# Recurrent attention: one fp32 exponential on ScalarE, and both fp16 terms of it made on VectorE

## The chip, the cores and the metric

The kernel runs on one core of a Trainium2 chip. The metric is the device time of one execution in microseconds. Three runs of the kernel before gave 709.27 to 709.52 us, median 709.41 us.

## The reference, cut to what matters

The whole program is a chain of six layers on 8 sequences of 32 tokens of 128 features. The change is in the fourth, an LSTM whose every step attends over a context of 512 rows:

```
def attend(h):
    q = h @ Wq.T
    scores = einsum('bc,bsc->bs', q, context)
    alpha = softmax(scores)
    ctx = einsum('bs,bsc->bc', alpha, context)
    return tanh(concat([ctx, h]) @ Wout.T + b_out)

def step(carry, x_t):
    h, c, attn = carry
    gates = concat([x_t, attn]) @ W_ih.T + b_ih + h @ W_hh.T + b_hh
    i, f, g, o = split(gates, 4)
    c = sigmoid(f) * c + sigmoid(i) * tanh(g)
    h = sigmoid(o) * tanh(c)
    attn = attend(h)
```

Each of the 32 time steps needs the attention output of the step before it, so the steps can't run side by side.

## The kernel before

**Two streams.** The 8 sequences are split into two streams of 4 (`g` = 0 and 1). `lstm_loop` (line 308) alternates them: one half step (a call of `half`) does the attention of one stream (`main`), the last part of the attention output of the other (`out`), and the LSTM gates of that other stream's next time step (`gates`). There are 64 half steps with a `main`. The first few are written out; then a hardware loop (line 319) runs 15 turns of four half steps each; two more follow. Inside the loop the wait values depend on the loop register, so some waits have a register instruction (REGISTER_ALU or ISA) ahead of them. The order on each engine is the order of the code; nothing is scheduled by a planner.

**Numbers in two terms.** TensorE works on fp16. A value that needs more precision is kept as two fp16 terms, a high one and the rest: `hsp` holds the terms of h, `asp` those of the attention output, `esp` those of the exponentials of the scores (index 0 the high term, 1 the rest). The exponentials of one half step are 128 x 16.

**One half step, on its engines.**
- TensorE (line 1617): 32 products of context keys with h, the scores (`scores(0)`, which raises `s_hi`, then `scores(1)`); a small product that turns the maxima `mc` (waits `m_c`); 12 products of the other stream's attention output with the gate weights (`output_gates`, waits `at_hi`, `at_lo`); one that subtracts the maximum (waits `m_d`, raises `s_ps`); gate products that need only x and h; then, after a wait on `e_hi`, the 16 products `values(1, 1)` of the context values with the high term of the exponentials; after a wait on `e_lo`, the sum of the exponentials over partitions (raises `z_ps`) and the 16 products `values(0, 2)` with both terms (raise `v_ps`). The next half step's scores follow directly.
- VectorE (line 1109): L1114, L1115 and L1126 turn the value sums of the other stream into `opre`, with L1120, the reduction of the new scores to `mc`, standing between L1115 and L1126 and waiting on `s_hi`. Then L1128 and L1130 make the two terms `asp` (after ScalarE's tanh), L1136 and L1138 prepare the maximum and the summed scores `ssum`, L1145 to L1152 do the LSTM cell, L1157 makes the second term of the exponentials, L1163 to L1166 make the terms of h, L1171 to L1175 the reciprocal of the softmax sum.
- ScalarE (line 656 on): L662 and L664 tanh of `opre`, L670 tanh of the gates, L676 the exponential of `ssum` written as fp16 into `esp` (raises `e_hi`), L678 the same exponential written as fp32 into `e32` (raises `e_32`), L683 tanh of the cell.

Of the kernel before, what the change touches and what calls it, by code (L numbers as in the profile page):

```python
# [17 lines left out]
ACT = mybir.ActivationFunctionType  # L18
# [85 lines left out]
def pat(t, dims, off=0):  # L104

    return bass.AP(tensor=t.tensor, offset=t.offset + off, ap=[list(t.ap[0])] + [list(d) for d in dims])
# [21 lines left out]
def build(nc, arr, out, upto=99):  # L128

    with ExitStack() as ctx:  # L130
        def sb(name, shape, dt=F32):
            return ctx.enter_context(nc.sbuf_tensor(name, shape, dt))

        sem = {}
# [12 lines left out]
        def v(name, i=0, n=1):  # L147
            return vec[:, V_AT[name] + i:V_AT[name] + i + n]
# [69 lines left out]
        lexp, lgate, loh = (sb(n, [P, 1]) for n in ("lexp", "lgate", "loh"))  # L218
# [10 lines left out]
        esp = sb("esp", [P, 2, 2, BH * KC], F16)  # L229
# [119 lines left out]
        def nth(stream, t):  # L349

            return t * 2 + (stream + 1)
# [143 lines left out]
        def _(act):  # L495
# [97 lines left out]
            for j in range(NJ):  # L593
                act.wait_ge(sem["a_pv"], j + 1)
                for half in range(2 - j):
                    act.activation(T[:, 8 + 2 * j + half, :], bank[2 + 2 * j + half][:, :], ACT.Copy) \
                       .then_inc(sem["a_oT"], 1)
# [50 lines left out]
            for g in range(4):  # L648
                act.wait_ge(sem["l_gxps"], g + 1)
                share = bank[g][:, 0:TOK].rearrange("p (b t) -> p b t", b=B)  # L650
                for to in (gx32[:, 0:1, g * B:(g + 1) * B], gx[:, 0:1, 0, g, :]):
                    ins = act.activation(to_time(to), share, ACT.Identity, bias=gbias[:, g:g + 1],
                                         scale=lgx[:, g // 3:g // 3 + 1])
# [3 lines left out]
            def half(main=None, out=None, gates=None):  # L657
                if out:

                    g, t = out  # L660
                    act.wait_ge(sem["o_pre"], nth(g, t))
                    act.activation(a32[:, g, :], opre[:, g, :], ACT.Tanh).then_inc(sem["at_32"], 1)  # L662
                    t = bass.ds(t, 1)
                    act.activation(yT[:, g * BH:(g + 1) * BH, t].rearrange("p b t -> p (b t)"), opre[:, g, :], ACT.Tanh) \  # L664
                       .then_inc(sem["y_st"], 1)
                if gates:

                    g, t = gates
                    act.wait_ge(sem["g_ps"], nth(g, t))
                    act.activation(gact[:, g, :], bank[GATES[g]][:, 0:4 * BH], ACT.Tanh, scale=lgate[:, :]) \  # L670
                       .then_inc(sem["g_act"], 1)
                if main:

                    g, t = main
                    act.wait_ge(sem["s_sum"], nth(g, t))
                    act.activation(esp[:, g, 0, :], ssum[:, g, :], ACT.Exp, scale=lexp[:, :]) \  # L676
                       .then_inc(sem["e_hi"], 1)
                    act.activation(e32[:, g, :], ssum[:, g, :], ACT.Exp, scale=lexp[:, :]) \  # L678
                       .then_inc(sem["e_32"], 1)
                if gates:  # L680
                    g, t = gates
                    act.wait_ge(sem["c_new"], nth(g, t))
                    act.activation(tanhc[:, g, :], c2[:, g, :], ACT.Tanh, scale=0.5).then_inc(sem["c_tanh"], 1)  # L683

            act.wait_ge(sem["l_zero"], L_ZEROED)
            lstm_loop(act, half)


# [80 lines left out]
        def _(dve):  # L769
# [326 lines left out]
            def parts(t, n, k):  # L1096

                return pat(t, [[1, n], [n, k]])
# [10 lines left out]
            def half(main=None, out=None, gates=None):  # L1109
                if out:  # L1110

                    g, t = out
                    dve.wait_ge(sem["v_ps"], nth(g, t))
                    step(dve.tensor_reduce(opre[:, g, :], parts(bank[6][:, 0:1], BH, 2), AX, ALU.add))  # L1114
                    step.mark(dve.tensor_tensor(opre[:, g, :], opre[:, g, :], rz[:, g, :], ALU.mult))  # L1115
                if main:

                    g, t = main
                    dve.wait_ge(sem["s_hi"], nth(g, t))
                    dve.tensor_reduce(mc[:, g, :], bank[1][:, 0:BH * KC].rearrange("p (b c) -> p b c", c=KC), AX, ALU.max) \  # L1120
                       .then_inc(sem["m_c"], 1)
                if out:

                    g, t = out
                    step.sync()
                    dve.tensor_tensor(opre[:, g, :], opre[:, g, :], oh[:, g, :], ALU.add).then_inc(sem["o_pre"], 1)  # L1126
                    dve.wait_ge(sem["at_32"], nth(g, t))
                    dve.tensor_scalar(asp[:, g, 0, :], a32[:, g, :], UNIT, None, ALU.mult).then_inc(sem["at_hi"], 1)  # L1128
                    dve.wait_ge(sem["at_hi"], nth(g, t))
                    dve.scalar_tensor_tensor(out=asp[:, g, 1, :], in0=a32[:, g, :], scalar=UNIT, in1=asp[:, g, 0, :],  # L1130
                                             op0=ALU.mult, op1=ALU.subtract).then_inc(sem["at_lo"], 1)
                if main:

                    g, t = main
                    dve.wait_ge(sem["m_t"], nth(g, t))
                    dve.tensor_reduce(m1[0:BH, g:g + 1], bank[3][0:BH, 0:P], AX, ALU.max).then_inc(sem["m_d"], 1)  # L1136
                    dve.wait_ge(sem["s_ps"], nth(g, t))
                    dve.tensor_reduce(ssum[:, g, :], pat(bank[1][:, 0:1], [[1, BH * KC], [BANK, 2], [BH * KC, 2]]),  # L1138
                                      mybir.AxisListType.XY, ALU.add).then_inc(sem["s_sum"], 1)
                if gates:  # L1140

                    g, t = gates
                    dve.wait_ge(sem["g_act"], nth(g, t))
                    i, f, o, gg = (gact[:, g, k * BH:(k + 1) * BH] for k in range(4))
                    step.mark(dve.scalar_tensor_tensor(out=fc2[:, g, :], in0=f, scalar=1.0, in1=c2[:, g, :],  # L1145
                                                       op0=ALU.add, op1=ALU.mult))
                    step.mark(dve.scalar_tensor_tensor(out=ig[:, g, :], in0=i, scalar=1.0, in1=gg,
                                                       op0=ALU.add, op1=ALU.mult))
                    step.sync()
                    dve.scalar_tensor_tensor(out=c2[:, g, :], in0=fc2[:, g, :], scalar=0.5, in1=ig[:, g, :],  # L1150
                                             op0=ALU.mult, op1=ALU.add).then_inc(sem["c_new"], 1)
                    step.mark(dve.tensor_scalar(o1[:, g, :], o, 1.0, UNIT, ALU.add, ALU.mult))  # L1152
                if main:

                    g, t = main
                    dve.wait_ge(sem["e_32"], nth(g, t))
                    dve.tensor_tensor(esp[:, g, 1, :], e32[:, g, :], esp[:, g, 0, :], ALU.subtract).then_inc(sem["e_lo"], 1)  # L1157
                if gates:

                    g, t = gates  # L1160
                    dve.wait_ge(sem["c_tanh"], nth(g, t))
                    step.sync()
                    dve.tensor_tensor(hsp[:, g, 0, :], o1[:, g, :], tanhc[:, g, :], ALU.mult).then_inc(sem["h_hi"], 1)  # L1163
                    step(dve.tensor_tensor(h32[:, g, :], o1[:, g, :], tanhc[:, g, :], ALU.mult))
                    dve.wait_ge(sem["h_hi"], nth(g, t))
                    dve.tensor_tensor(hsp[:, g, 1, :], h32[:, g, :], hsp[:, g, 0, :], ALU.subtract).then_inc(sem["h_lo"], 1)  # L1166
                if main:

                    g, t = main
                    dve.wait_ge(sem["oh_ps"], nth(g, t))  # L1170
                    step.mark(dve.tensor_scalar(oh[:, g, :], bank[5][:, 0:BH], loh[:, :], v("bout"), ALU.mult, ALU.add))  # L1171
                    dve.wait_ge(sem["z_ps"], nth(g, t))
                    step(dve.tensor_reduce(zs[:, g, :], pat(bank[4][:, 0:1], [[KC, BH], [BH * KC, 2], [1, KC]]),  # L1173
                                           mybir.AxisListType.XY, ALU.add))
                    step(dve.reciprocal(rz[:, g, :], zs[:, g, :]))  # L1175


            for t, x in ((two, 2.0), (shifts[0], SHIFTS[0]), (shifts[1], SHIFTS[1]), (one, 1.0)):
                dve.memset(t, x).then_inc(sem["m_setup"], 1)
            lstm_loop(dve, half, step)  # L1180
            dve.wait_ge(sem["y_tr"], 1)
            dve.tensor_tensor(xres[:, :, :], xres[:, :, :], bank[7][:, 0:TOK].rearrange("p (j d) -> p j d", j=NJ),  # L1182
# [756 lines left out]
```

## Time and profile before

| | us |
|---|---|
| median of three runs | 709.41 |
| the profiled execution's own time | 708.04 |
| its span, first to last instruction | 706.2 |
| TensorE busy | 574.1 (81%) |
| VectorE busy | 478.9 (68%) |
| ScalarE busy | 299.5 (42%) |
| GpSimd busy | 161.7 (23%) |

The recurrent layer fills the span from about 234 to 478 us. Two durations of neighbours on one engine may overlap in these rows: the next instruction can start before the one ahead of it has delivered its last element, so what an instruction costs its engine is the distance between starts, and what it costs a reader on another engine is its full duration and the step to that reader's start.

### The profile page before, as it was taken

What the parts mean: (1) busy time and instruction counts of PE and PEld (TensorE: products, weight loads), DVE (VectorE), ACT (ScalarE), POOL (GpSimd) and SP (SyncE); (2) the same over time, 40 slices, a digit from 0 to 9 for tenths busy, and PEclk for the clock granted to TensorE, in tenths of its full rate; (3) what the DMA queues carried; (4) which work ended last, traced back from release to release, by engine and by line L of the source; (5) the groups of instructions that cost most, each with busy time, mean ns of one, the idle gap of its engine ahead of it and who ended that gap; (6) DMA issues with size and microseconds to landing.
All of it is one profiled execution on the core that took longest, in us unless ns stands there. A gap on an engine that the chain in (4) does not pass through costs nothing.

```text
span 706.2 us, 21667 instructions
## 1 busy us (share of the span) xinstructions
PE 574.1 (81%) x8501; PEld 449.5 (64%) x8501; DVE 478.9 (68%) x1894; ACT 299.5 (42%) x851; POOL 161.7 (23%) x208
## 2 busy tenths in 40 slices
PE   3958758569995699999899999886788988898866
PEld 2625534357884688888888888875456656665634
DVE  1568649964444677777777777771588888978783
ACT  2868725224565333333233233233545444555411
POOL 2245533117000000000000000001564356336600
PEclk9989979796997555555555555555799999999997
DMA  8800000010002000000000000000000000000000
GB/s 341 354 1 2 1 3 1 2 41 3 1 1 90 3 3 0 0 0 0 0 0 0 0 0 0 0 1 0 1 0 1 1 0 1 1 0 1 1 0 7
DMA packets 6057, 15.26 MB, mean 22 GB/s; under 512 B 2641, under 2 KB 3289, under 8 KB 5505
## 3 DMA queue, kind: packets, MB, share of 16 engines
q1 hardware_dynamic: 5296, 11.19, 4.3%
q10 hardware_dynamic: 720, 3.55, 1.3%
q8 instruction: 24, 0.39, 0.2%
q14 instruction: 17, 0.13, 0.1%
HBM read 14.60 MB, written 0.13 MB: 21 GB/s over the span
## 4 chain that ended last, share of the span: by engine, by line
PE 41%; DVE 33%; ACT 13%; issue 10%; DMA 1%; DVEq 1%; POOL 0%; SPq 0%; ACTq 0%; POOLq 0%
PE bank L1678 9%; PE bank L1751 7%; PE bank L1587 6%; ACT esp L676 3%; PE bank L1538 2%; DVE ssum L1138 2%; ACT a L662 2%; DVE T L1208 2%; ACT e L678 2%; PE bank L1525 2%; DVE rz L1175 2%; DVE zs L1173 2%; DVE asp L1128 2%; DVE opre L1114 2%; ACT T L546 1%
## 5 line engine op out<-in xcount | busy, mean ns | idle before, releaser
L472 POOL MEMSET ctxT<- 128x128 f32 x1 | 0.3, 312 | 305.8 <-DVE xres L1182 305.8
L1587 PE MATMUL bank<-esp,qblk 128*128 128x1 f16 (+1 forms) x2048 | 66.5, 166 | 0.8 <-ACT esp L676 0.8
L1587 PE MATMUL bank<-hsp,kT 128*128 128x2 f16 x2048 | 63.5, 166 | 2.3 <-DVE hsp L1166 1.7
L1587 PEld LDWEIGHTS bank<-esp,qblk 128*128 128x128 f16 x2048 | 61.2, 104 | 1.4 <-ACT esp L676 1.1
L662 ACT ACTIVATE a<-opre 128x4 f32<-128x4 f32 x64 | 13.1, 205 | 115.2 <-DVE opre L1126 115.2
L1587 PEld LDWEIGHTS bank<-hsp,kT 128*128 128x128 f16 x2048 | 59.9, 104 | 3.1 <-DVE hsp L1163 1.7
L1208 DVE SCALAR_TENSOR_TENSOR T<-bank,bct,T 128x256 f32<-128x256 f32 x112 | 46.4, 476 | 1.3 <-PE bank L1764 1.3
L1195 DVE TENSOR_TENSOR_SCAN qblk<-ctxT,bank 128x512 f32<-128x512 f32 x32 | 37.6, 1208 | 13.2 <-PE bank L1751 13.2
L1587 PE MATMUL bank<-asp,lsp 128*128 128x4 f16 x768 | 30.7, 168 | 16.3 <-DVE asp L1128 16.3
L1195 DVE TENSOR_TENSOR_SCAN w<-kT,bank 128x512 f32<-128x512 f32 x32 | 37.6, 1208 | 8.4 <-PE bank L1751 8.4
L1587 PEld LDWEIGHTS bank<-asp,lsp 128*128 128x128 f16 x768 | 25.4, 105 | 27.8 <-DVE asp L1128 27.7
L670 ACT ACTIVATE gact<-bank,lgate 128x16 f32<-128x16 f32 x64 | 17.5, 274 | 45.6 <-PE bank L1587 45.6
L1751 PE MATMUL bank<-maskb,T 128*128 128x512 f32 x64 | 35.3, 675 | 0.5 <-ACT T L740 0.5
L1587 PE MATMUL bank<-hsp,lsp 128*128 128x4 f16 x984 | 35.4, 166 | 0.0
L1751 PE MATMUL bank<-w,T 128*128 128x512 f32 x64 | 34.6, 655 | 1.0 <-DVE w L1195 1.0
L1587 PE MATMUL bank<-gx,T 128*128 (+1 forms) x198 | 27.8, 191 | 6.5 <-DVE gx L1107 6.5
L1587 PEld LDWEIGHTS bank<-hsp,lsp 128*128 128x128 f16 x984 | 32.0, 105 | 0.0
L490 POOL TENSOR_TENSOR kT<-T,aneg 128x496 f32<-128x496 f32 x32 | 31.2, 1012 | 3.3 <-DVE T L1265 3.3
L490 POOL TENSOR_TENSOR ctxT<-T,aneg 128x496 f32<-128x496 f32 x32 | 31.2, 1012 | 3.1 <-DVE T L1265 3.1
L546 ACT ACTIVATE T<-T,xneg 128x512 f32<-128x512 f32 x32 | 23.0, 720 | 11.4 <-DVE xneg L848 11.3
L419 POOL TENSOR_SCALAR T<-T,xrz 128x512 f32<-128x512 f32 x32 | 22.2, 694 | 22.3 <-DVE xrz L854 22.3
L484 POOL TENSOR_TENSOR maskb<-cst,bct 128x512 f32<-128x512 f32 x16 | 16.1, 1040 | 47.9 <-ACT bct L729 47.9
(326 smaller groups left out, 1410.5 us busy)
## 6 DMA issues: line engine op xcount, KB each, us to landing
w<-in_w_dram SPq DMA_DIRECT2D x2, 2048.0 KB
ctxT<-in_ctxT_dram SPq DMA_DIRECT2D x8, 256.0 KB, 13.4
wqkv<-in_qkvT_dram ACTq DMA_DIRECT2D x1, 1536.0 KB, 12.2
w<-in_mw_dram SPq DMA_DIRECT2D x1, 1024.0 KB, 5.1
lw<-in_lw_dram SPq DMA_DIRECT2D x1, 960.0 KB, 19.8
rows<-in_rows_dram ACTq DMA_DIRECT2D x1, 772.0 KB, 8.2
wqkv<-in_fw_dram SPq DMA_DIRECT2D x1, 532.0 KB, 3.4
T<-in_mask_dram ACTq DMA_DIRECT2D x1, 512.0 KB, 6.2
```

What stands on the lines that cost most here:

```text
L419: pool.tensor_scalar(x_soft(i), x_soft(i), xrz[:, i:i + 1], 0.0, ALU.mult, ALU.add).then_inc(sem["x_norm"], 1)
L484: pool.tensor_tensor(diagb[s][:, ng * 512:(ng + 1) * 512].rearrange("p (n t) -> p n t", t=P), pat(ident, [[0, NG], [1, P]]), pat(bct[:, s, ...
L490: pool.tensor_tensor(tile(c, i), pat(delta, [[0, NG], [S, BT], [1, S - 1]], ch * P + 1), pat(aneg[:, :], [[1, NG], [0, BT], [0, S - 1]], ( ...
L546: act.activation(x_soft(i), x_soft(i), ACT.Exp, scale=-1.0, bias=xneg[:, i:i + 1], accum_out=xz[:, i:i + 1]).then_inc(sem["x_exp"], 1)
L662: act.activation(a32[:, g, :], opre[:, g, :], ACT.Tanh).then_inc(sem["at_32"], 1)
L670: act.activation(gact[:, g, :], bank[GATES[g]][:, 0:4 * BH], ACT.Tanh, scale=lgate[:, :]) \
L676: act.activation(esp[:, g, 0, :], ssum[:, g, :], ACT.Exp, scale=lexp[:, :]) \
L1195: dve.tensor_tensor_scan(out=hid[q % 2][:, at], data0=decay[q % 2][:, at], data1=bank[i % 4][:, :], initial=0.0, op0=ALU.mult, op1=ALU.add ...
L1208: ins = dve.scalar_tensor_tensor(out=cacc[n % 2], in0=hT, scalar=c_n, in1=cacc[n % 2], op0=ALU.mult, op1=ALU.add)
L1587: return pe.matmul(out, lhsT, rhs, start=start, stop=stop, skip_group_check=True)
L1678: return pe.matmul(out, lhsT, rhs, start=start, stop=stop, skip_group_check=True)
L1751: pe.matmul(bank[i % 4][:, :], duT[s][:, ch * P:(ch + 1) * P], diagb[s][:, ng * 512:(ng + 1) * 512], start=True, stop=True).then_inc(sem[" ...
```

## The change

ScalarE no longer writes the fp16 exponential itself. It takes the fp32 exponential alone; VectorE casts it to fp16 into the high term of `esp` (raising `e_hi` itself), waits for that cast, and subtracts it from the fp32 value as before. TensorE's program and its waits are unchanged.

```
@@ ScalarE, half() @@
                     g, t = main
                     act.wait_ge(sem["s_sum"], nth(g, t))
-                    act.activation(esp[:, g, 0, :], ssum[:, g, :], ACT.Exp, scale=lexp[:, :]) \
-                       .then_inc(sem["e_hi"], 1)
                     act.activation(e32[:, g, :], ssum[:, g, :], ACT.Exp, scale=lexp[:, :]) \
                        .then_inc(sem["e_32"], 1)
@@ VectorE, half() @@
                     g, t = main
                     dve.wait_ge(sem["e_32"], nth(g, t))
+                    dve.tensor_copy(esp[:, g, 0, :], e32[:, g, :]).then_inc(sem["e_hi"], 1)
+                    dve.wait_ge(sem["e_hi"], nth(g, t))
                     dve.tensor_tensor(esp[:, g, 1, :], e32[:, g, :], esp[:, g, 0, :], ALU.subtract).then_inc(sem["e_lo"], 1)
```

Two lines go from ScalarE's part, so lines 678 to 1155 of the kernel before have numbers smaller by two in the new one; from L1157 on both agree.

On ScalarE, inside the loop, between the gates' tanh (`gact`) and the cell's (`tanhc`), the kernel before has:

```order
L670 ACTIVATE gact<-bank,lgate 128x16 [waits g_ps]
L676 ACTIVATE esp<-ssum,lexp 128x16 [waits s_sum]
L678 ACTIVATE e32<-ssum,lexp 128x16
L683 ACTIVATE tanhc<-c2 128x4 [waits c_new]
L662 ACTIVATE a32<-opre 128x4 [waits o_pre]
```

and the changed one:

```order
L670 ACTIVATE gact<-bank,lgate 128x16 [waits g_ps]
L676 ACTIVATE e32<-ssum,lexp 128x16 [waits s_sum]
L681 ACTIVATE tanhc<-c2 128x4 [waits c_new]
L662 ACTIVATE a32<-opre 128x4 [waits o_pre]
```

One activation is gone; the other three keep their order and waits.

On VectorE, at the same place of the half step (the LSTM cell, the terms of the exponentials, the terms of h), the kernel before has:

```order
L1150 SCALAR_TENSOR_TENSOR c2<-fc2,ig 128x4 [waits dve_step]
L1152 TENSOR_SCALAR o1<-gact 128x4
L1157 TENSOR_TENSOR esp<-e32,esp 128x16 [waits e_32]
L125 REGISTER_ALU [waits c_tanh]
L1163 TENSOR_TENSOR hsp<-o1,tanhc 128x4 [waits dve_step]
```

and the changed one:

```order
L1148 SCALAR_TENSOR_TENSOR c2<-fc2,ig 128x4 [waits dve_step]
L1150 TENSOR_SCALAR o1<-gact 128x4
L1155 CAST esp<-e32 128x16 [waits e_32]
L1157 TENSOR_TENSOR esp<-e32,esp 128x16 [waits e_hi]
L125 REGISTER_ALU [waits c_tanh]
L1163 TENSOR_TENSOR hsp<-o1,tanhc 128x4 [waits dve_step]
```

The cast stands between the cell's last operation and the subtraction, which now waits for the cast; no register instruction is added.

## Rows read from the trace of the kernel before

**Rows 1.** Busy time in the stretch that the loop fills.
```profile
core 0: us, PE busy (x) PEld busy (x) DVE busy (x) ACT busy (x) POOL busy (x), PEclk, DMA share, GB/s
246.00:471.00 225.00, 204.03 (x5781) 187.31 (x5779) 165.38 (x1133) 71.40 (x359) 0.00 (x0) 0.50 0.00 0
```

**Rows 2.** Chain that ended last, one half step: start us, us, what.
```profile
402.93 0.31 ACT esp L676
403.23 0.21 ACT e L678
...
404.83 0.07 DVE opre L1115
```

**Rows 3.** Timeline of the same half step: start us, us, engine, line, what.
```profile
402.67 0.23 DVE L1138 TENSOR_REDUCE ssum<-bank 128x16 f32<-128x64 f32 x1 [0.29 <-PE bank L1587]
...
402.83 0.54 PE L1587 MATMUL bank<-hsp,lsp 128*128 128x4 f16 x15
...
403.14 0.29 ACT L678 ACTIVATE e<-ssum,lexp 128x16 f32<-128x16 f32 x1
403.14 0.16 DVE L1150 SCALAR_TENSOR_TENSOR c<-fc,ig 128x4 f32<-128x4 f32 x1
403.22 0.16 DVE L1152 TENSOR_SCALAR o<-gact 128x4 f32<-128x4 f32 x1
...
403.29 0.58 PE L1587 MATMUL bank<-esp,qblk 128*128 128x1 f16 x16
403.34 0.21 ACT L683 ACTIVATE tanhc<-c 128x4 f32<-128x4 f32 x1
403.46 0.18 DVE L1157 TENSOR_TENSOR esp<-e,esp 128x16 f16<-128x16 f32 x1
403.66 0.16 DVE L1163 TENSOR_TENSOR hsp<-o,tanhc 128x4 f16<-128x4 f32 x1
...
404.24 0.99 PE L1587 MATMUL bank<-hsp,kT 128*128 128x2 f16 x32
...
404.91 0.17 DVE L1120 TENSOR_REDUCE mc<-bank 128x4 bf16<-128x16 f32 x1
405.03 0.16 DVE L1126 TENSOR_TENSOR opre<-opre,oh 128x4 f32<-128x4 f32 x1
...
405.46 0.17 DVE L1128 TENSOR_SCALAR asp<-a 128x4 f16<-128x4 f32 x1 [0.27 <-ACT a L662]
...
405.69 0.48 PE L1587 MATMUL bank<-asp,lsp 128*128 128x4 f16 x12 [0.26 <-DVE asp L1128]
...
406.31 0.23 DVE L1138 TENSOR_REDUCE ssum<-bank 128x16 f32<-128x64 f32 x1 [0.29 <-PE bank L1587]
```

**Rows 4.** Timeline of a half step written out before the loop.
```profile
241.21 0.58 PE L1587 MATMUL bank<-esp,qblk 128*128 128x1 f16 x16 [0.19 <-ACT esp L676]
```

**Rows 5.** VectorE operations nearest to the cast, all of each form: busy, mean ns.
```profile
L1010 DVE CAST i8f<-i 128x16 f32<-128x16 uint32 x2 | 0.3, 174 | 0.1
L945 DVE COPY ltop<-lmax 128x3 f32<-128x3 f32 x1 | 0.2, 169 | 0.0
```

**Rows 6.** Timeline of the first half step.
```profile
235.24 0.99 PE L1587 MATMUL bank<-hsp,kT 128*128 128x2 f16 x32 [1.69 <-DVE hsp L1166]
235.85 0.17 DVE L1120 TENSOR_REDUCE mc<-bank 128x4 bf16<-128x16 f32 x1 [0.75 <-PE bank L1587]
```

**Rows 7.** Timeline across one loop turn.
```profile
366.35 0.99 PE L1587 MATMUL bank<-hsp,kT 128*128 128x2 f16 x32
...
367.43 0.17 DVE L1120 TENSOR_REDUCE mc<-bank 128x4 bf16<-128x16 f32 x1
```

**Rows 8.** Line 1120: who waited for it in the whole program, us and times.
```profile
  PEld bank L1587: 6.0, 16
```

More of the change, by code:

```diff
@@ L675, in half @@
                     act.wait_ge(sem["s_sum"], nth(g, t))
-                    act.activation(esp[:, g, 0, :], ssum[:, g, :], ACT.Exp, scale=lexp[:, :]) \
-                       .then_inc(sem["e_hi"], 1)
                     act.activation(e32[:, g, :], ssum[:, g, :], ACT.Exp, scale=lexp[:, :]) \
@@ L1156, in half @@
                     dve.wait_ge(sem["e_32"], nth(g, t))
+                    dve.tensor_copy(esp[:, g, 0, :], e32[:, g, :]).then_inc(sem["e_hi"], 1)
+                    dve.wait_ge(sem["e_hi"], nth(g, t))
                     dve.tensor_tensor(esp[:, g, 1, :], e32[:, g, :], esp[:, g, 0, :], ALU.subtract).then_inc(sem["e_lo"], 1)
```

## The prediction

> **What bounds the kernel now.** I read the busy time by stretch first. In the loop TensorE is busy 204.03 of 225.00 us, VectorE 165.38, ScalarE only 71.40, and TensorE's granted clock is 0.50, its 1.2 GHz level [rows 1]. ScalarE, which is to be relieved, is the idlest of the three, so what its operation costs has to be read from the order of events in one half step.
>
> The chain of waits runs from the summed scores `ssum` through both exponentials (0.31 and 0.21 us) and on through VectorE to L1115 [rows 2]. A learner may conclude that a shorter ScalarE part shortens the chain. But the chain shows only the tightest path; the timeline shows how close the next one is, and that is TensorE. One half step lasts from 402.67 to 406.31, 3.64 us [rows 3]. In it:
> - TensorE starts the first value products at 403.29. The fp16 exponential ended at 402.93 + 0.31 = 403.24 [rows 2], so they start 0.05 us after it, and the 15 gate products ahead of them end issuing at about the same moment (they start at 402.83, 32 score products issue in under 1 us, some 0.03 us each, so 15 take 0.46) [rows 3]. In a half step written out ahead of the loop TensorE did stand 0.19 us waiting for this exponential [rows 4]. `e_hi` has no slack.
> - From there TensorE works without a pause to the next scores at 404.24, 0.95 us later [rows 3].
> - VectorE's L1120 starts at 404.91, 0.67 us after the scores start [rows 3]. In the first half step, where L1120 really waited for TensorE, that distance was 0.61 us (235.24 to 235.85) [rows 6]. So TensorE's path has only 0.06 us of slack against VectorE's here.
> - L1126 stands behind L1120 in VectorE's queue, and on it hang ScalarE's tanh, L1128 (405.46), the output gates (405.69) and the next `ssum` (406.31) [rows 3].
>
> **What is removed.** One exponential of 16 columns per half step. The fp32 one now starts when `ssum` is there, at 402.93 instead of 403.14, and with its 0.29 us ends at 403.22 instead of 403.43 [rows 2, 3]. The cell's tanh (403.34) gets nothing: its input `c2` ends at 403.14 + 0.16 = 403.30 and the usual step to a reader brings it to 403.33 [rows 3]. So ScalarE gives back 0.01 us at most there, 0.6 us over 64 half steps; I count it as nothing, as the wait is on `c2` in both.
>
> **What is added.** One cast on VectorE in each of 64 half steps, and a wait of VectorE on itself.
>
> The cast can't start at 403.25, when its input is there: L1152 starts at 403.22 ahead of it. Neighbours on this engine that need not wait for each other start 0.08 us apart (L1150 at 403.14, L1152 at 403.22) [rows 3], so it starts at 403.30. Its length isn't in the trace; the nearest rows are a copy with 169 ns and a cast of the same 16 columns with 174 ns, and the shortest VectorE rows near it have 0.16 [rows 3, 5]. I take 0.17, bounds 0.155 and 0.175. It ends at 403.47, and with 0.05 us to TensorE (as from the exponential; from L1128 to the output gates it is 0.06) [rows 3] the value products start at 403.52 instead of 403.29: **0.23 us later**. That is the point: the high term that TensorE waits for now goes through two engines in series instead of one.
>
> The Trainium skill has a price for the cast ("VectorE: DVE Perf Modes", section "The TRN2 errata"): 58 cycles and half a cycle per fp32 column at 0.96 GHz, here about 0.07 us; that is an estimate from that page, which says itself that its fixed part is too low for a single operation, and the rows of 169 and 174 ns agree with that caveat. By this price the delay would be 0.13 us, and the result 3.4 us instead of the 8.2 below.
>
> The subtraction waits for the cast and starts about 0.20 us after it, as L1163 stands 0.20 after L1157 (a dependent or held start) [rows 3], at 403.50 instead of 403.46. Behind it is L1163, which needs the tanh (end 403.55) and a register instruction; it starts at 403.66 if the tanh decides, at 403.70 if it keeps its 0.20 us from the subtraction [rows 3]. So VectorE's own chain loses 0 to 0.04 us. `e_lo` comes at 403.50 + 0.18 + 0.05 = 403.73, TensorE wants it only at about 403.97 (403.52 plus 16 products of 0.03): no new wait.
>
> **What is late next.** The next scores start at 404.24 + 0.23 = 404.47; with the 0.61 us L1120 can start at 405.08 instead of 404.91, now waiting for TensorE. L1115 (404.83 [rows 2], up to 404.87 now) is no longer what it stands behind. L1126 comes 0.12 us after L1120 as before [rows 3], at 405.20 instead of 405.03, and everything behind it keeps its distance: 0.17 us per half step. This last 0.12 is partly the wait for L1115; with that gone it may be 0.08 (two free neighbours), and with a register instruction executed behind a late wait up to 0.20, the distance of L1163 to L1157. That gives 0.155 - 0.04 = 0.115 us per half step as the low bound and 0.175 + 0.08 = 0.255 us as the high one.
>
> **Where it is covered.** At each turn of the loop VectorE's branch is slower than TensorE's: the scores start at 366.35 and L1120 only at 367.43, 1.08 us later [rows 7], so 0.47 us of slack over 0.61 takes the whole 0.23. TensorE waited for L1120 16 times, 6.0 us together [rows 8]: the 14 turns back, the entry, and the exit. There I charge nothing (0.04 x 16 = 0.6 us if VectorE's own chain is longer by its upper bound).
>
> **The sum.** 64 - 16 = 48 half steps x 0.17 = 8.2 us longer; nothing is hidden elsewhere, since the layers behind the loop start from its result, and there neither order nor work changes. The profiled execution takes 708.04 us, 1.4 us less than the median of the runs (709.41); it would go to 716.2, and the runs to **717.6 us**. The bounds give 48 x 0.115 = 5.5 and 48 x 0.255 + 0.6 = 12.8 us, so 714.9 to 722.2 us.
>
> **Rivals.**
> 1. *TensorE's delay stays covered.* The half step is bound by VectorE's chain alone, as the chain of waits says, and `s_hi` is not on the edge. For it: L1120 is never recorded as waiting for TensorE in the loop. Against: the 0.61 us of the first half step. Its price is 0 to 0.04 us x 64 = 0 to 2.6 us: about 710.7 us. It decides if the true distance from scores to L1120 is below 0.44 us.
> 2. *Faster.* The tanh of the cell was held by the second exponential rather than by `c2`, L1163 and all of VectorE's chain move up, and TensorE has more slack than I read. The place is ScalarE's L683, which starts 0.20 us after L678 [rows 3]; freed, it could move by the 0.01 us above, or 0.05 if the step from `c2` is shorter than I take it: up to 64 x 0.05 = 3.2 us, 706.2 us. It needs the cast's 0.23 us on TensorE to be covered as in rival 1 as well.
> 3. *The cast is held until L1152 has finished*, so that it starts at 403.38, 0.08 us later: 0.25 us per half step, 48 x 0.25 = 12.0, 721.4 us. The rows speak against it: L1152 starts 0.08 after L1150, which lasts 0.16 [rows 3]. The Trainium skill states this rule as well ("VectorE: DVE Perf Modes", section "The DRAIN you can't avoid": the next operation does not start before the pipe is empty), and adds that one which isn't held may start earlier; the rows agree with the addition.
> 4. *The cast is short*, 0.07 us or so: 48 x 0.07 = 3.4 us, 712.8 us. No VectorE row near it is under 0.15.
>
> **How the numbers follow.** The forecast has a chance of 0.80; rival 1 0.08, rival 2 0.03, rival 3 0.05, rival 4 0.04. The range leaves out rivals 1, 2 and 4 and the last of the high bound: 714.0 to 721.0 us. It starts below 714.9 because the last half steps have no L1152 ahead of the cast. A difference of 0.2% (1.4 us) is what a measurement of this kernel tells from none. Slower by more: the forecast, rivals 3 and 4 and half of rival 1, 0.93. Within: half of rival 1, 0.04. Faster: 0.03.
>
> **What would show it.** In the profile of the changed kernel, in a half step inside the loop: the value products some 0.85 us after `ssum` starts (0.62 before); TensorE idle about 0.2 us ahead of them, released by the cast; L1120's successor idle and waiting for TensorE, 0.61 us after the scores start; the tanh of `opre` 0.17 us later within the half step; a half step of 3.81 us, but the one across a loop turn as long as before, to 0.04 us. If the half step grows while VectorE shows no wait for TensorE at the score reduction, the reasoning is wrong even if the time is right. If the value products start less than 0.1 us later, the cast is cheaper than its neighbours.

## The result: 4.4 us slower, half of what was forecast

The changed kernel takes 713.35 us (median of 8 runs), the kernel before 708.99 us (median of 8), a ratio of 1.006 with a 95% interval of 1.0045 to 1.0074. The forecast was 717.6 us, 714.0 to 721.0. The sign was right, the size twice too large, and the range missed by 0.65 us.

A warning on spans first. The profiled execution of the changed kernel has a span of 713.6 us, 7.4 more than before, but it was the slowest of its eight runs (715.47 us). Its first `ssum` comes at 239.39 us against 237.04, so 2.35 us of the difference lie in layers that did not change. From the first `ssum` to the last it takes 241.84 us (239.39 to 481.23), and the kernel before 237.14 (237.04 to 474.18): 4.70 us more, which is what the change costs in the recurrence.

Below is the timeline of one half step inside the loop of the changed kernel, as in [rows 3] (start us, us, engine, line, operation).

```profile
404.71 0.23 DVE L1136 TENSOR_REDUCE ssum<-bank 128x16 f32<-128x64 f32 x1 [0.29 <-PE bank L1587]
...
404.97 0.31 ACT L676 ACTIVATE e<-ssum,lexp 128x16 f32<-128x16 f32 x1
...
405.27 0.16 DVE L1150 TENSOR_SCALAR o<-gact 128x4 f32<-128x4 f32 x1
405.34 0.17 DVE L1155 CAST esp<-e 128x16 f16<-128x16 f32 x1
405.38 0.20 ACT L681 ACTIVATE tanhc<-c 128x4 f32<-128x4 f32 x1
405.54 0.18 DVE L1157 TENSOR_TENSOR esp<-e,esp 128x16 f16<-128x16 f32 x1
405.56 0.59 PE L1587 MATMUL bank<-esp,qblk 128*128 128x1 f16 x16
405.71 0.16 DVE L1163 TENSOR_TENSOR hsp<-o,tanhc 128x4 f16<-128x4 f32 x1
...
406.47 0.99 PE L1587 MATMUL bank<-hsp,kT 128*128 128x2 f16 x32
...
406.91 0.16 DVE L1113 TENSOR_TENSOR opre<-opre,rz 128x4 f32<-128x4 f32 x1
407.07 0.17 DVE L1118 TENSOR_REDUCE mc<-bank 128x4 bf16<-128x16 f32 x1
407.17 0.16 DVE L1124 TENSOR_TENSOR opre<-opre,oh 128x4 f32<-128x4 f32 x1
...
407.83 0.48 PE L1587 MATMUL bank<-asp,lsp 128*128 128x4 f16 x12 [0.18 <-DVE asp L1126]
...
408.45 0.22 DVE L1136 TENSOR_REDUCE ssum<-bank 128x16 f32<-128x64 f32 x1 [0.29 <-PE bank L1587]
```

From one `ssum` to the next there are 3.74 us (404.71 to 408.45), where there were 3.64. The value products start 0.85 us after `ssum`, as forecast. The scores follow 0.91 us later (0.95 before), `mc` (now L1118) 0.60 later (0.67 before), the addition to `opre` (now L1124) 0.10 later (0.12 before). The multiplication ahead of `mc` (L1113) starts 0.16 us before it; before the change that distance was 0.08 (L1115 at 404.83, L1120 at 404.91 [rows 2, 3]). These 0.08 us are VectorE's new wait for the scores.

The chain that ended last in another half step (start us, us, what) now leaves VectorE after the cast and runs over 33 of TensorE's products, where it ran through the second exponential before [rows 2]:

```profile
409.17 0.09 DVE esp L1155
409.25 0.05 issue
409.30 1.05 PE bank L1587 x33
```

What the whole execution says of the cast, all 64 together (duration min/median/max, first and last start), and of those who waited for the `esp` tile (us, times):

```profile
L1155 DVE CAST esp<-e x64: 165/167/175, 240.0 to 481.8; 128x16 f16<-128x16 f32 x64
...
  PEld bank L1587: 15.1, 64
```

TensorE's weight loads now wait for it in all 64 half steps, 0.24 us each. At a loop turn the length has not moved: the timeline shows the scores and `mc` 0.88 us apart, the `ssum` rows 4.17 us (4.17 to 4.18 before).

```profile
369.81 0.23 DVE L1136 TENSOR_REDUCE ssum<-bank 128x16 f32<-128x64 f32 x1 [0.29 <-PE bank L1587]
...
371.70 0.99 PE L1587 MATMUL bank<-hsp,kT 128*128 128x2 f16 x32
...
372.58 0.17 DVE L1118 TENSOR_REDUCE mc<-bank 128x4 bf16<-128x16 f32 x1
...
373.98 0.23 DVE L1136 TENSOR_REDUCE ssum<-bank 128x16 f32<-128x64 f32 x1 [0.29 <-PE bank L1587]
```

### The profile page after: what moved, and what is told of

Read it like the earlier page. It is cut to its first block, busy times and chain, and to the rows that moved or that the text cites. A ratio compares the mean times of both kernels' runs of the same rounds, so it can differ in the third digit from the quotient of the medians.

```text
span 713.6 us, 21667 instructions
## 1 busy us (share of the span) xinstructions
PE 579.7 (81%) x8501; PEld 449.0 (63%) x8501; DVE 485.7 (68%) x1958; ACT 293.2 (41%) x787; POOL 162.0 (23%) x208
## 3 DMA queue, kind: packets, MB, share of 16 engines
q10 hardware_dynamic: 720, 3.55, 1.3%
## 4 chain that ended last, share of the span: by engine, by line
PE 47%; DVE 30%; ACT 11%; issue 9%; DMA 1%; DVEq 1%; POOL 0%; SPq 0%; ACTq 0%; POOLq 0%
PE bank L1587 12%; PE bank L1678 9%; PE bank L1751 7%; ACT gact L670 2%; PE bank L1538 2%; ACT a L662 2%; DVE T L1208 2%; PE bank L1525 2%; DVE asp L1126 2%; DVE opre L1112 2%; DVE opre L1124 2%; DVE c L1148 1%; DVE opre L1113 1%; DVE ig L1145 1%; ACT T L546 1%
## 5 line engine op out<-in xcount | busy, mean ns | idle before, releaser
L1136 DVE TENSOR_REDUCE ssum<-bank 128x16 f32<-128x64 f32 x64 | 14.4, 225 | 18.6 <-PE bank L1587 18.6
```

## The experiments

The table gives, for each kernel, the median position of five starts after `ssum` over the ordinary half steps of the loop, that is those that no loop turn stands in (read from the timeline; us), the length of such a half step, and the ratio to the kernel before in the runs, with its 95% interval. "2nd h term" is L1166, on which `h_lo` hangs.

| kernel | value products | 2nd h term | scores | mc | add to opre | half step | ratio |
|---|---|---|---|---|---|---|---|
| before | 0.62 | 1.26 | 1.57 | 2.24 | 2.36 | 3.64 | 1 |
| changed | 0.85 | 1.27 | 1.75 | 2.35 | 2.45 | 3.74 | 1.006 (1.0045 to 1.0074) |
| 1 exponentials swapped | 0.82 | 1.27 | 1.72 | 2.33 | 2.42 | 3.71 | 1.0065 (1.0037 to 1.0092) |
| 2 unused copy | 0.62 | 1.26 | 1.57 | 2.25 | 2.36 | 3.65 | 1.0001 (0.9973 to 1.0028) |
| 3 cast earlier | 0.83 | 1.27 | 1.74 | 2.34 | 2.44 | 3.72 | 1.0056 (1.0032 to 1.0080) |
| 4 two links | 1.06 | 1.40 | 1.96 | 2.56 | 2.66 | 3.94 | 1.0247 (1.0221 to 1.0272) |
| 5 no fp32 exponential | 0.62 | 1.27 | 1.58 | 2.25 | 2.36 | 3.65 | 0.9995 (0.9978 to 1.0013) |
| 6 changed, addition first | 0.85 | 1.27 | 1.75 | 2.47 | 2.39 | 3.67 | 1.0033 (1.0011 to 1.0055) |
| 7 before, addition first | 0.62 | 1.26 | 1.58 | 2.45 | 2.37 | 3.65 | 1.0004 (0.9976 to 1.0031) |
| 8 before, late wait for rz | 0.62 | 1.27 | 1.57 | 2.18 | 2.28 | 3.56 | 0.9867 (0.9823 to 0.9910) |
| 9 before, both orders | 0.62 | 1.26 | 1.57 | 2.29 | 2.21 | 3.50 | 0.9848 (0.9820 to 0.9876) |
| 10 changed, both orders | 0.85 | 1.27 | 1.76 | 2.41 | 2.33 | 3.61 | 0.9926 (0.9898 to 0.9954) |
| 11 filled | 0.76 | 1.27 | 1.64 | 2.25 | 2.37 | 3.65 | 0.9998 (0.9976 to 1.0021) |
| 12 before, h late | 0.62 | 1.36 | 1.66 | 2.33 | 2.45 | 3.73 | 1.0110 (1.0067 to 1.0153) |
| 13 changed, h late | 0.84 | 1.36 | 1.75 | 2.35 | 2.45 | 3.73 | 1.0097 (1.0063 to 1.0131) |

### Is it TensorE's later start, or VectorE's extra operation? (1 to 4)

**1, the exponentials swapped.** The fp16 exponential comes late, but no cast exists.

```
 act.wait_ge(sem["s_sum"], nth(g, t))
+act.activation(e32[:, g, :], ssum[:, g, :], ACT.Exp, ...).then_inc(sem["e_32"], 1)
 act.activation(esp[:, g, 0, :], ssum[:, g, :], ACT.Exp, ...).then_inc(sem["e_hi"], 1)
-act.activation(e32[:, g, :], ssum[:, g, :], ACT.Exp, ...).then_inc(sem["e_32"], 1)
 ...
 dve.wait_ge(sem["e_32"], nth(g, t))
+dve.wait_ge(sem["e_hi"], nth(g, t))
```

> The kernel before, with the two exponentials of ScalarE in the other order: fp32 first, fp16 second, and no cast on VectorE. Theory A (the added time is TensorE's later start at the high term): the fp16 exponential ends 0.21 us later, the value products start 0.83 us after ssum instead of 0.62, and the ordinary half step in the loop is 0.83 + 2.88 = 3.71 us instead of 3.64, where 2.88 is the rest of the half step as the changed kernel shows it (3.74 less 0.85); about 3.5 us more than before in all. Theory B (the added time is VectorE's extra operation and its wait on itself): 3.64 us, same time as before.

3.71 us, as theory A says to the hundredth, and a ratio of 1.0065. The timeline of one half step of this kernel:

```profile
402.91 0.23 DVE L1138 TENSOR_REDUCE ssum<-bank 128x16 f32<-128x64 f32 x1 [0.29 <-PE bank L1588]
...
403.73 0.59 PE L1588 MATMUL bank<-esp,qblk 128*128 128x1 f16 x16
...
404.64 0.99 PE L1588 MATMUL bank<-hsp,kT 128*128 128x2 f16 x32
...
405.34 0.16 DVE L1126 TENSOR_TENSOR opre<-opre,oh 128x4 f32<-128x4 f32 x1
...
406.62 0.22 DVE L1138 TENSOR_REDUCE ssum<-bank 128x16 f32<-128x64 f32 x1 [0.29 <-PE bank L1588]
```

No operation was added anywhere, and the runs don't tell this kernel from the changed one (1.0065 and 1.006). In the traces it takes 3.44 us more than the kernel before from the first `ssum` to the last, the changed one 4.70; its value products are 0.03 us less late. A late high term is enough.

**2, an unused copy** of the same 16 columns in the place of the cast, on the kernel before.

```
 g, t = main
+dve.wait_ge(sem["s_sum"], nth(g, t))
+dve.tensor_copy(ecopy[:, g, :], ssum[:, g, :])
 dve.wait_ge(sem["e_32"], nth(g, t))
```

> The kernel before, with one more VectorE copy of 16 columns from ssum to an unused fp16 tile ahead of the subtraction; both exponentials stay on ScalarE. Theory A: the copy fits between L1152 and the subtraction, TensorE waits for nothing new, the half step stays at 3.64 us, within 0.02. Theory B: VectorE is the bound and pays the 0.08 us between two starts: 3.72 us, 5 us more in all.

3.65 us and no difference in the runs: the operation, which starts 0.61 us after `ssum` and lasts 0.17, costs at most 0.01 us on VectorE. Theory B falls with 1 and 2.

**3, the cast ahead of `o1`.** The two lines of the cast's wait and the cast stand ahead of `step.mark(dve.tensor_scalar(o1...))`.

> The changed kernel with the cast ahead of the gate operation o1 instead of behind it. Theory A: the cast starts 0.58 us after ssum instead of 0.63, the value products at 0.80 instead of 0.85, and the half step is 3.68 to 3.69 us instead of 3.74: about 2.3 us less than the changed kernel. Theory B: the same number of VectorE operations in another order, 3.74 us.

The cast starts at 0.60, not 0.58, so the products start at 0.83, and the half step is 3.72: the direction of A, with 0.02 us of the 0.05 to 0.06 expected, because the input of the cast arrives 0.02 us later than I had reckoned. In the runs this is within the scatter of the changed kernel.

**4, two links.**

```
-dve.tensor_copy(esp[:, g, 0, :], e32[:, g, :]).then_inc(sem["e_hi"], 1)
+dve.tensor_copy(ecopy[:, g, :], e32[:, g, :]).then_inc(sem["e_cp"], 1)
+dve.wait_ge(sem["e_cp"], nth(g, t))
+dve.tensor_copy(esp[:, g, 0, :], ecopy[:, g, :]).then_inc(sem["e_hi"], 1)
```

> The changed kernel with a second link in the chain: an fp32 copy of e32 on VectorE, a wait for it, and then the cast to fp16. Theory A: the value products start 0.20 us later again, 1.05 us after ssum, with no cover left: half step 1.05 + 2.88 = 3.93 us; the half step across a loop turn, covered so far, pays up to 0.2 us because VectorE's own chain is longer too. About 12 us more than the changed kernel. Theory B: one more start to start distance, 0.08 to 0.10 us, half step 3.83 us, 5 to 6 us more.

3.94 us against 3.93 expected, and a ratio of 1.0247, 17 us more than before. In the kernels 1, 3, 4 and the changed one the half step is the start of the value products plus 2.88 or 2.89 us. It is a line with slope one: past the slack nothing hides the delay.

### Did ScalarE's relief give anything back? (5)

This kernel leaves out the second term of the exponentials.

```
-act.activation(e32[:, g, :], ssum[:, g, :], ACT.Exp, ...).then_inc(sem["e_32"], 1)
 ...
-dve.wait_ge(sem["e_32"], nth(g, t))
-dve.tensor_tensor(esp[:, g, 1, :], e32[:, g, :], esp[:, g, 0, :], ALU.subtract)...
+dve.wait_ge(sem["e_hi"], nth(g, t))
+dve.tensor_tensor(esp[:, g, 1, :], esp[:, g, 0, :], esp[:, g, 0, :], ALU.subtract)...
```

> What ScalarE's relief is worth by itself: the kernel before without its fp32 exponential, and without the cast. The second fp16 term isn't computed (it becomes zero). ScalarE has one exponential per half step, e_hi comes as early as before. If VectorE's L1163 is released by the cell's tanh, which waits for c2, nothing moves up: 3.64 us, same time as before, within 0.02 us. The rival (the second exponential and the subtraction hold the chain, as the chain of waits shows them) gives up to 0.2 us less, 3.44 us and 9 us in all.

3.65 us, ratio 0.9995. The subtraction moves up from 0.80 to 0.62 us after `ssum`, and its successor stays where it was and now shows the wait that had been there all along. The timeline of this kernel:

```profile
404.33 0.22 DVE L1136 TENSOR_REDUCE ssum<-bank 128x16 f32<-128x64 f32 x1 [0.29 <-PE bank L1585]
...
404.96 0.16 DVE L1155 TENSOR_TENSOR esp<-esp 128x16 f16<-128x16 f16 x1
405.33 0.16 DVE L1161 TENSOR_TENSOR hsp<-o,tanhc 128x4 f16<-128x4 f32 x1 [0.21 <-ACT tanhc L681]
```

The chain of waits of the kernel before put 0.21 us on the second exponential [rows 2]; taking it away is worth nothing, as the tanh of the cell arrives no earlier. A chain names one path among equals.

### Where does the lateness turn into time? (6 to 10)

**6 and 7, the addition ahead of `mc`** in VectorE's queue, on the changed kernel and, as a control, on the one before:

```
 step.mark(dve.tensor_tensor(opre[:, g, :], opre[:, g, :], rz[:, g, :], ALU.mult))
+step.sync()
+dve.tensor_tensor(opre[:, g, :], opre[:, g, :], oh[:, g, :], ALU.add).then_inc(sem["o_pre"], 1)
 dve.wait_ge(sem["s_hi"], nth(g, t))
 dve.tensor_reduce(mc[:, g, :], ..., AX, ALU.max).then_inc(sem["m_c"], 1)
-step.sync()
-dve.tensor_tensor(opre[:, g, :], opre[:, g, :], oh[:, g, :], ALU.add).then_inc(sem["o_pre"], 1)
```

> The changed kernel with VectorE's addition to opre (released to ScalarE's tanh) ahead of the score maximum mc in the queue, instead of behind it. If the late scores cost time only because the addition stands in the queue behind a reduction that waits for them, the addition no longer moves with them: it follows L1113 (2.20 us after ssum) by 0.20 us, at 2.40 instead of 2.45, and the half step is 3.69 us instead of 3.74, some 2.3 us less in all. If TensorE's lateness costs the time by itself, whatever stands in VectorE's queue, the half step stays at 3.74 us.

> The kernel before with the addition to opre ahead of mc in VectorE's queue, and nothing else. The addition waits 0.20 us for the multiplication in either order (2.16 to 2.36 us after ssum), so the half step stays at 3.64 us, within 0.02: with the scores in time, the order is worth nothing. A gain of over 0.03 us would mean that the order helps by itself and that the gain of the same edit in the changed kernel says nothing on the cast.

3.67 us on the changed kernel (3.74 without it), 3.65 on the one before (3.64). The edit is worth nothing where the scores are in time and takes over half of the loss away where they are late: from the first `ssum` to the last the changed kernel takes 4.70 us more than the one before, kernel 6 only 2.01. (The runs alone give 1.006 and 1.0033, with intervals that overlap.) So most of the price is paid in VectorE's queue: an addition that doesn't need the scores stands behind a reduction that does. What is left of the loss (0.03 us) lies in the value sums that come later: L1112 starts 2.00 us after `ssum` (L1114 of the kernel before 1.96), the multiplication 2.20 against 2.16. In every third ordinary half step of kernel 6 the multiplication is another 0.02 to 0.04 us later, and the half step is 3.70 us. In the changed kernel it is 0.02 to 0.04 us later at the same place, which costs nothing there, as `mc` has to wait for the scores anyway. Where that small delay comes from wasn't looked for.

**8, 9 and 10, the wait for the reciprocal moved** to the multiplication that uses it, alone on the kernel before (8), with the addition first (9), and both on the changed kernel (10):

```
-step(dve.reciprocal(rz[:, g, :], zs[:, g, :]))
+step.mark(dve.reciprocal(rz[:, g, :], zs[:, g, :]))
```

`step` waits at once for what it issues, `step.mark` leaves the wait to the next `step`, which here is the reduction of the value sums, still ahead of the multiplication.

> The kernel before with the reciprocal's completion waited for only ahead of the multiplication, and the addition behind mc as before. L1114 starts at 1.85 us after ssum, the multiplication at 2.02, but mc now waits for the scores: 1.57 + 0.60 = 2.17, the addition at 2.27: half step 3.55 to 3.56 us, between the kernel before (3.64) and the same with the addition first (3.50), which is the 0.06 to 0.07 us of slack of the scores showing as a wait. If mc is not held by the scores here, it is 3.51 us.

> The kernel before with two changes of VectorE's order of waiting: the addition to opre ahead of mc, and the reciprocal's completion waited for only ahead of the multiplication that uses it, so that L1114 can start when the value sums are there. If VectorE's own chain is what binds the kernel before at 3.64 us, L1114 starts at 1.83 us after ssum (0.08 behind the reciprocal) instead of 1.96, the multiplication at 2.03, the addition at 2.23 instead of 2.36: half step 3.51 us, about 6 us less than before in all. If TensorE's path to the value sums binds as well, the gain is under half of it.

> The changed kernel with the same two changes of VectorE's order. The value sums come 0.2 us later here (the scores behind them start at 1.75 us after ssum, not 1.57), so L1112 can't start before some 1.95 us; multiplication 2.15, addition 2.35: half step 3.63 us, about as long as the kernel before, and 0.12 us more than the same order without the cast. If the cast's delay of TensorE no longer mattered in this order, it would be 3.51 us too.

3.56, 3.50 and 3.61 us, against 3.55 to 3.56, 3.51 and 3.63 expected. Kernel 9 takes 697.82 us, 1.5% less than before and the fastest here; with the cast it is 703.30 us. So in the faster order the change costs more, 0.11 us per half step and 5.5 us in all: VectorE reduces the value sums at 1.85 us in kernel 9 (1.96 before), so there is less in which TensorE's delay can hide, and at 1.93 us in kernel 10. The timeline of kernel 9:

```profile
406.00 0.23 DVE L1141 TENSOR_REDUCE ssum<-bank 128x16 f32<-128x64 f32 x1 [0.29 <-PE bank L1590]
...
407.57 0.99 PE L1590 MATMUL bank<-hsp,kT 128*128 128x2 f16 x32
407.85 0.14 DVE L1114 TENSOR_REDUCE opre<-bank 128x4 f32<-128x8 f32 x1
408.02 0.16 DVE L1115 TENSOR_TENSOR opre<-opre,rz 128x4 f32<-128x4 f32 x1
408.22 0.16 DVE L1120 TENSOR_TENSOR opre<-opre,oh 128x4 f32<-128x4 f32 x1
408.30 0.17 DVE L1125 TENSOR_REDUCE mc<-bank 128x4 bf16<-128x16 f32 x1
...
409.50 0.23 DVE L1141 TENSOR_REDUCE ssum<-bank 128x16 f32<-128x64 f32 x1 [0.29 <-PE bank L1590]
```

### Why was the loss 0.10 us and not 0.17? (11 to 13)

The largest missing part is the way from value products to scores: 0.95 us before, 0.90 with the change.

**11, filled.** Seven more products ahead of the value products, so that TensorE gets to them late without waiting.

```
+for _ in range(7):
+    mm(bank[5][:, BH:2 * BH], weight(0, 8), hsp[:, g, 0, :], start=True, stop=True)
 for k, n in MEETS:
     ins = mm(bank[5][:, 0:BH], weight(k, 8), hsp[:, g, n, :], ...)
```

> The kernel before with 7 more products of h with weights (into an unused part of a bank) ahead of the value products, so that these start about as late as with the cast (0.83 to 0.85 us after ssum) but TensorE works up to them instead of waiting. Theory A alone: 0.84 + 2.88 = 3.72 us per half step, whatever makes them late. Theory C (the 0.05 us by which values and scores take 0.90 us instead of 0.95 in the changed kernel is an address or wait computation of TensorE's queue, hidden when the queue has run ahead during a wait): no wait, so 0.95 us, scores at 1.79, half step 3.77 us. 3.72 or less would leave C without support.

Two things came out otherwise. The filling was worth less than planned: 22 products from 405.06 to 405.65 are 0.027 us each, not 0.031, so the value products start at 0.76. And the scores follow 0.88 us behind them with no wait in between, so theory C has no support. The timeline:

```profile
404.89 0.23 DVE L1138 TENSOR_REDUCE ssum<-bank 128x16 f32<-128x64 f32 x1 [0.29 <-PE bank L1587]
...
405.06 0.73 PE L1587 MATMUL bank<-hsp,lsp 128*128 128x4 f16 x22
405.65 0.56 PE L1587 MATMUL bank<-esp,qblk 128*128 128x1 f16 x16
...
406.17 0.16 DVE L1166 TENSOR_TENSOR hsp<-h,hsp 128x4 f16<-128x4 f32 x1
...
406.53 0.99 PE L1587 MATMUL bank<-hsp,kT 128*128 128x2 f16 x32
...
408.54 0.22 DVE L1138 TENSOR_REDUCE ssum<-bank 128x16 f32<-128x64 f32 x1 [0.29 <-PE bank L1587]
```

It also measures the slack directly: scores 0.07 us later than before, half step 0.01 longer. And it led to another reading. At 0.027 us each, the 15 gate products of the kernel before are issued by 0.56, so by this estimate TensorE did wait some 0.06 us for the exponential. And in every kernel whose scores start at 1.57 or 1.58, the second term of h starts at 1.26 or 1.27, 0.31 us earlier; the same 0.31 stands in the first half step, where the scores plainly waited for it (L1166 at 234.93, scores at 235.24). The scores of the kernel before might wait too, for VectorE.

**12 and 13, the terms of h later**, by three unused copies, on the kernel before and on the changed one:

```
-step(dve.tensor_tensor(h32[:, g, :], o1[:, g, :], tanhc[:, g, :], ALU.mult))
+step.mark(dve.tensor_tensor(h32[:, g, :], o1[:, g, :], tanhc[:, g, :], ALU.mult))
+for k in range(3):
+    dve.tensor_copy(spare[:, k, :], o1[:, g, :])
+step.sync()
```

> The kernel before with three small unused copies on VectorE between the fp32 h (L1164) and its second fp16 term (L1166), so that the terms of h come about 0.13 us later. Theory D (the scores of the kernel before are held by the second term of h, 0.31 us after its start, and not by TensorE's own work, which is what makes the value products to scores 0.95 us there and 0.90 in the changed kernel): the term of h starts at 1.40 us after ssum instead of 1.26, the scores at 1.70 to 1.71 instead of 1.57, 1.09 us behind the value products. Theory E (TensorE's own queue takes 0.95 us there): scores at 1.57 to 1.60. Both expect a longer half step of about 3.77 us, since VectorE's own chain is 0.13 us longer.

> The same three copies in the changed kernel. Theory D: TensorE is ready for the scores at 1.75 us after ssum and the term of h is there for it from 1.27 + 0.13 + 0.31 = 1.71, so the scores stay at 1.75, 0.90 us behind the value products. Theory E gives the same here. If the scores move by the 0.13 us as well, the 0.31 us is not a fixed distance and theory D falls. Half step about 3.78 us by VectorE's own chain.

The delay came out as 0.10 us, not 0.13. On the kernel before the scores went with it, from 1.57 to 1.66, while the value products stayed at 0.62. The timeline of kernel 12, an ordinary half step and the scores of another one early in the loop:

```profile
404.52 0.23 DVE L1139 TENSOR_REDUCE ssum<-bank 128x16 f32<-128x64 f32 x1 [0.29 <-PE bank L1591]
...
405.15 0.59 PE L1591 MATMUL bank<-esp,qblk 128*128 128x1 f16 x16
...
405.88 0.15 DVE L1170 TENSOR_TENSOR hsp<-h,hsp 128x4 f16<-128x4 f32 x1
406.18 1.00 PE L1591 MATMUL bank<-hsp,kT 128*128 128x2 f16 x32
```

```profile
254.48 0.16 DVE L1170 TENSOR_TENSOR hsp<-h,hsp 128x4 f16<-128x4 f32 x1
...
254.79 0.99 PE L1591 MATMUL bank<-hsp,kT 128*128 128x2 f16 x32 [0.31 <-DVE hsp L1170]
```

In that one the second term of h came at 1.67 us instead of 1.36, the scores at 1.98, and here the profile itself names L1170 as what TensorE waited for.

On the changed kernel they did not move. The timeline of kernel 13:

```profile
403.94 0.23 DVE L1137 TENSOR_REDUCE ssum<-bank 128x16 f32<-128x64 f32 x1 [0.29 <-PE bank L1591]
...
404.78 0.59 PE L1591 MATMUL bank<-esp,qblk 128*128 128x1 f16 x16
...
405.29 0.15 DVE L1170 TENSOR_TENSOR hsp<-h,hsp 128x4 f16<-128x4 f32 x1
405.68 0.99 PE L1591 MATMUL bank<-hsp,kT 128*128 128x2 f16 x32
```

406.18 is 0.30 us after the term of h; 405.68 is 0.39 after it and 0.90 after the value products. Theory D holds: the scores start at the later of two times, value products plus 0.88 to 0.91, and second term of h plus 0.30 to 0.31. And both kernels have the same half step, 3.73 us (in kernel 12 every third ordinary one is 3.80, as its second term of h comes later by itself, at 1.41 to 1.44 us, and the scores with it): with VectorE's own chain 0.10 us longer, the cast costs nothing.

The trace of the kernel before had shown this already, in a half step written out ahead of the loop, the one of [rows 4]:

```profile
240.59 0.23 DVE L1138 TENSOR_REDUCE ssum<-bank 128x16 f32<-128x64 f32 x1 [0.29 <-PE bank L1587]
...
241.76 0.16 DVE L1166 TENSOR_TENSOR hsp<-h,hsp 128x4 f16<-128x4 f32 x1
...
242.11 0.99 PE L1587 MATMUL bank<-hsp,kT 128*128 128x2 f16 x32
```

There the second term of h starts at 1.17 us, early enough, and the scores follow the value products (241.21) after 0.90 us, not 0.95. With the cast the scores of such a half step are the full 0.22 to 0.23 us later, and the two of them are 0.15 and 0.16 us longer (3.55 and 3.56 to 3.70 and 3.72), near the 0.17 of the forecast.

## Why the prediction was wrong in size and right in kind

- **The value products 0.23 us later: right.** 0.62 to 0.85. The cast has a median of 167 ns for the 0.17 taken and starts 0.63 us after `ssum`. The price for it in the Trainium skill ("VectorE: DVE Perf Modes", section "The TRN2 errata"), about 0.07 us as an estimate, doesn't hold for this cast. What that page adds, that its fixed part is too low for a single operation, agrees with the 167 ns.
- **ScalarE's relief worth nothing: right**, by kernel 5. Rival 2 is out.
- **VectorE's own chain longer by 0 to 0.04 us: right.** L1163 starts at 1.00 us after `ssum` for 0.99.
- **"From there TensorE works without a pause to the next scores": wrong**, and the step that failed. TensorE paused about 0.05 us before the scores, for the second term of h (kernels 12 and 13). That much of the new delay is hidden: the scores went from 1.57 to 1.75, 0.18 us and not 0.23. The pause could not be seen as idle time, as each product is recorded with 0.166 us while the next can start 0.027 later; a wait under some 0.14 us stays inside the last product's bar.
- **"L1120's successor idle and waiting for TensorE": not there as written.** The profile lists L1118 as waiting for TensorE in one half step only, as it did L1120 before, and by the prediction's own sign the reasoning would then be wrong. The wait is there all the same, 0.08 us long, but inside the bar of the multiplication ahead of it: the starts are 0.16 us apart instead of 0.08, while the bar lasts 0.16. That it costs time is shown by kernels 6 and 7, not by an idle time. The sign was badly chosen.
- **0.06 us of slack between the scores and `mc`: slightly small.** 0.67 became 0.60, so it was 0.07.
- **The addition 0.12 us after `mc`: too much.** With the wait for the multiplication gone it is 0.10. I had bounded it at 0.08 and kept the old value.
- Together: 0.17 forecast, less 0.05, 0.01 and 0.02, is 0.09; the trace has 2.36 to 2.45, and 3.64 to 3.74 in the half step.
- **Covered at 16 places: right for 15.** The half steps across a turn are 4.17 us as before, the exit 3.81 for 3.82. The entry paid 0.08 us (3.90 for 3.82).
- **The total.** 48 half steps of 0.09 to 0.10 us are 4.3 to 4.8 us, and the trace has 4.70, but this agreement is partly luck. The 4.70 us are 3.92 from the 42 ordinary half steps of the later turns (0.093 each), 0.31 from the two ahead of the loop, 0.08 from the entry, 0.50 from the three of the first turn, of which one alone has 0.31, less 0.11 at the turns and the exit.
- **The range.** Its low end came from bounds on the cast and on the last 0.12 us, not from the 0.95, for which I took no bound at all. A distance that two engines may decide needs one. The 713.35 us lie nearest to rival 4 (712.8 us), and that is chance, as its short cast isn't there.
- Rival 1 was half true. The slack that it needs (0.23) was not there, but 0.12 of it was, in two pieces on two engines (0.05 of TensorE before the scores, 0.07 of VectorE before `mc`). Rivals 3 and 4 are out by the cast's start (0.63 us after `ssum`, where rival 3 needs 0.71) and its length (0.167 us).

One thing stays open: one half step early in the loop is 3.95 us in the changed kernel and 3.64 before. There VectorE starts the multiplication 0.47 us after the reduction of the value sums, and 0.20 us in the half steps beside it. Kernel 2, which has no longer ordinary half step, has it too (3.90), and so have kernels 1, 3, 6 and 12 (3.92 to 4.04), so it isn't the cast's wait. It is 0.3 us once, and its cause wasn't looked for.

## What to carry to other kernels

In a recurrence the question of an edit is not which engine is relieved but which of the waiting engines gets its input later. A conversion put between a producer and a consumer makes the consumer's input later by its full length and a handover (0.17 + 0.05 us here), though its engine has room for it; what comes out of that in time is what the slack further on leaves over (0.10 of 0.23 us here). Where queues are in order, look at what stands behind the instruction that becomes late: moving one independent addition ahead of it, and waiting for a reciprocal only where it is used, was worth 1.5%, more than the change cost. Short operations that start before the one ahead has ended show no idle time even where they wait (0.05 us on TensorE, 0.08 on VectorE here). To know a slack, compare distances between starts with those of a half step that has no such wait, or delay the one thing by itself.

## What the runs showed of the hardware

- From the start of a VectorE operation of 0.16 us to the product that waits for it there were 0.30 to 0.31 us for the second term of h (the products have two waits ahead of them, `h_hi` and `h_lo`; the first half step, and kernel 12 with the term at 1.36, 1.42 and 1.67 us), but about 0.22 us for the cast (405.34 to 405.56) and 0.23 for L1126 (407.60 to 407.83 in the changed kernel). Why the first handover is longer by 0.08 us wasn't tried.
- Products of four columns start 0.027 us apart at the granted clock of 0.50 when nothing holds them (22 in 0.59 us in kernel 11), and products of one column 0.028 (16 in 0.45 us in the changed kernel).
